# Turning cached keys in 32x32 blocks on VectorE, and dividing by the row sums after P·V instead of before it

## The reference

```python
kc = k_cache[block_table].reshape(bsz, L, HK, D)
k_all = jnp.concatenate([kc, k], axis=1)
scores = jnp.einsum('bqhd,bkhd->bhqk', q, k_all) * SCALE
scores = jnp.where(valid[:, None, None, :], scores, -1e+30)
probs = jax.nn.softmax(scores, axis=-1)
o = jnp.einsum('bhqk,bkhd->bqhd', probs, v_all)
return jnp.einsum('bse,de->bsd', o.reshape(bsz, seqlen, HQ * D), Wo)
```

## Time and profile before

| | |
|---|---|
| median of 3 runs | 1533.02 us |
| the profiled execution, own time | 1530.62 us |
| its span | 1528.9 us |
| PE / VectorE / ScalarE / GpSimd busy | 94% / 76% / 61% / 32% of the span |
| mean granted TensorE clock | 0.992 |
| layer 1, its 66 steps | about 300 to 1466 us of the span |
| cached keys turned on PE | 256 matmuls, 38.7 us busy |
| P divided: ScalarE / VectorE | 128 x 0.824 us / 128 x 0.545 us |

### The profile page before, as it was taken

The page is one execution under the profiler, slowest core; times in us unless marked ns, Lnnn a source line. Parts: engine busy times, 40 slices in busy tenths (PEclk is TensorE's granted clock), DMA queues, the critical chain, the costliest instruction groups (busy, mean ns, idle before and its releaser), DMA issues.

```text
span 1528.9 us, 29324 instructions
## 1 busy us (share of the span) xinstructions
PE 1434.5 (94%) x8014; PEld 1230.2 (80%) x8014; DVE 1163.2 (76%) x2800; ACT 939.4 (61%) x1860; POOL 493.7 (32%) x678
## 2 busy tenths in 40 slices
PE   3998999788999899999999999999999999999988
PEld 2776887667788788888878887888788888888767
DVE  4675767566688788778878886888788778888756
ACT  2333232356677677767767776777677667777643
POOL 4243000155543333333433333343333333433200
PEclk9999999999999999999999999999999999999999
DMA  8678642345321112111111111021112111111214
GB/s 179 207 240 283 197 150 89 98 126 159 111 63 49 50 29 63 60 40 49 50 47 45 57 56 51 29 63 49 51 29 63 60 40 49 50 42 36 97 60 161
DMA packets 104275, 131.03 MB, mean 86 GB/s; under 512 B 11861, under 2 KB 79590, under 8 KB 98838
## 3 DMA queue, kind: packets, MB, share of 16 engines
q1 hardware_dynamic: 98678, 109.49, 23.6%
q0 software_dynamic: 5024, 17.93, 3.9%
q10 hardware_dynamic: 384, 1.41, 0.7%
HBM read 125.63 MB, written 36.72 MB: 106 GB/s over the span
## 4 chain that ended last, share of the span: by engine, by line
PE 75%; issue 9%; DVE 7%; ACT 2%; POOL 2%; DMA 2%; POOLq 1%; SPq 1%; ACTq 0%; DVEq 0%
PE proj_ps L1170 16%; PE sc L1210 12%; PE o_ps L1247 12%; PE proj_ps L1268 11%; PE ring L1229 8%; PE proj_ps L1026 4%; PE o_ps L1026 4%; PE sc L1026 3%; PE ring L1283 2%; PE ring L1295 1%; PE ring L1026 1%; DMA wd_raw<-in_WdT 1%; POOLq L584 1%; DVE w_l L1426 1%; POOL v_pages L585 1%
## 5 line engine op out<-in xcount | busy, mean ns | idle before, releaser
L1699 DVE TENSOR_TENSOR pTl<-ring,pTh 128x512 fp32r<-128x512 f32 x320 | 215.1, 689 | 72.8 <-ACT pTh L851 69.3
L833 ACT ACTIVATE p_sb<-p_sb,bias,rstd 128x640 f32<-128x640 f32 x256 | 235.8, 921 | 46.7 <-DVE bias L1675 46.7
L637 POOL TENSOR_TENSOR rstd<-var,half_neg 128x4 f32<-128x4 f32 x64 | 80.6, 1259 | 532.1 <-DVE var L1736 483.5
L851 ACT ACTIVATE pTh<-ring 128x512 fp32r<-128x512 f32 x320 | 184.4, 599 | 55.2 <-PE ring L1229 54.4
L1665 DVE CUSTOM_DVE_ANT_0 p_sb<-sc,mask 128x640 f32<-128x640 f32 x256 | 209.1, 817 | 4.4 <-PE sc L1210 0.8
L1229 PE MATMUL ring<-ident,p_sb 128*128 128x128 f32 x1280 | 183.5, 274 | 5.7 <-DVE p_sb L1691 3.4
L1170 PE MATMUL proj_ps<-wh,xh 128*128 128x512 f32 (+1 forms) x512 | 179.7, 351 | 8.9 <-issue 8.2
L1229 PEld LDWEIGHTS ring<-ident,p_sb 128*128 128x128 f32 x1280 | 153.9, 141 | 33.5 <-DVE p_sb L1691 3.7
L1170 PE MATMUL proj_ps<-wl,xh 128*128 128x512 f32 (+1 forms) x512 | 172.6, 337 | 0.0
L1170 PE MATMUL proj_ps<-wh,xl 128*128 128x512 f32 (+1 forms) x512 | 172.2, 336 | 0.0
L1210 PE MATMUL sc<-kTh,qTh 128*128 128x320 f32 x512 | 163.5, 319 | 1.8 <-DVE kTl L1800 1.8
(11 more groups left out here) (247 smaller groups left out, 3632.7 us busy)
## 6 DMA issues: line engine op xcount, KB each, us to landing
k_pages<-in_k_cache SPq DMA_DIRECT2D x128, 128.0 KB, 3.4
v_pages<-in_v_cache POOLq DMA_DIRECT2D x128, 128.0 KB, 3.5
k_raw<-k_pages SPq DMA_DIRECT2D x64, 256.0 KB, 3.1
v_raw<-v_pages SPq DMA_DIRECT2D x64, 256.0 KB, 3.0
stage<-in_Wqkv SPq DMA_DIRECT2D x32, 384.0 KB, 3.5
w_raw<-in_WguT SPq DMA_DIRECT2D x20, 512.0 KB, 5.7
stage<-in_WoT SPq DMA_DIRECT2D x32, 256.0 KB, 3.3
w_raw<-in_W3T SPq DMA_DIRECT2D x8, 1024.0 KB, 5.4
```

The source lines that it names most:

```text
L833: act_e.activation(p_sb[:, p_slot(u, h), :], p_sb[:, p_slot(u, h), :], ACT.Exp, bias=bias[:, h:h + 1], scale=rstd[:, u.k % 2, h:h + 1], ac ...
L851: act_e.activation(pTh[:, c, :], ring[c % 2][:, :], ACT.Copy).then_inc(S["pth"], 1)
L1699: v.tensor_tensor(pTl[:, c, :], ring[c % 2][:, :], pTh[:, c, :].bitcast(F32), ALU.subtract).then_inc(S["ptl"], 1)
```

## The change

The keys are loaded by four DMAs instead of one, so that key 32·i + c, dimension 32·j + r lies at partition 32·j + c, column 32·i + r: `k_raw` is [128, 512], and one 32x32 block-wise transpose on VectorE (`turn_cached_k`) gives the full transpose in `k_turned`. PE's `transpose_keys` is gone, its semaphore `kcT` now comes from VectorE; the low part of the cached keys moves from VectorE to GpSimd. P is no longer divided: `invert` makes one reciprocal of four columns, SyncE writes it to DRAM with heads and tokens swapped and reads it back onto all partitions (`spread_inv`), and VectorE multiplies the unit's `o_ps` by that row (`norm_o`) into `o_sb`, which shares memory with `q_sin`. `oTh` and `oTl` are made from `o_sb`.

SyncE, `load_k`, `spread_inv` and `step`:

```diff
-                sp.dma_start(k_raw[:, :, :], of_head(k_pages, u)).then_inc(k_load, 16)
+                pages = k_pages[u.seq, :, :, :].rearrange("(i r) h d -> r i (h d)", r=PSIZE)
+                for j in range(D // PSIZE):
+                    sp.dma_start(k_raw[j * PSIZE:(j + 1) * PSIZE, :].rearrange("r (i c) -> r i c", c=PSIZE),
+                                 pages[:, :, bass.ds(u.head * D + j * PSIZE, PSIZE)]).then_inc(k_load, 16)
...
+            def spread_inv(u):
+                if not u.exists():
+                    return
+                par = u.k % 2
+                sp.wait_ge(S["inverted"], u.count(1, 1))
+                sp.dma_start(inv_dram[par].rearrange("h t -> t h"), inv[:, par, :],
+                             allow_slow_non_contiguous=True).then_inc(S["inv_put"], 16)
+                sp.wait_ge(S["inv_put"], u.count(16, 16))
+                sp.dma_start(inv_row[:, :], inv_dram[par].rearrange("h t -> (h t)").partition_broadcast(P)
+                             ).then_inc(S["inv_in"], 16)
...
                 if u.exists() and (u.turn is not None or u.k > 0):
                     load_k(u)
+                spread_inv(u + -2)
                 load_in(u + 4, 0)
```

GpSimd, `turn_and_norm`:

```diff
+                if u.back(3):
+                    pool.wait_ge(S["ol"], (u + -3).count(1, 1))
...
+                pool.wait_ge(S["kch"], u.count(1, 1))
+                pool.tensor_tensor(kTl[:, u.k % 2, 0:L], k_turned[:, :], kTh[:, u.k % 2, 0:L].bitcast(F32), ALU.subtract
+                                   ).then_inc(S["kcl"], 1)
                 pool.wait_ge(S["q_var"], u.count(1, 1))
```

ScalarE (both `normalise` calls are gone, and `high_cached_k` stands ahead of `square_q`):

```diff
-                act_e.wait_ge(S["pv"], u.count(KC, KC))
+                act_e.wait_ge(S["on"], u.count(1, 1))
...
-                act_e.activation(oTh[:, :], o_ps[:, :], ACT.Copy).then_inc(S["oh"], 1)
+                act_e.activation(oTh[:, :], o_sb[:, :], ACT.Copy).then_inc(S["oh"], 1)
...
-                act_e.activation(kTh[:, u.k % 2, 0:L], ring[1][:, :], ACT.Copy).then_inc(S["kch"], 1)
+                act_e.activation(kTh[:, u.k % 2, 0:L], k_turned[:, :], ACT.Copy).then_inc(S["kch"], 1)
```

PE (`transpose_keys` is gone):

```diff
-                    pe.wait_ge(S["normed_v"], u.count(2, 2))
-                    pe.wait_ge(S["normed_s"], u.count(2, 2))
+                    pe.wait_ge(S["exped"], u.count(REP, REP))
```

VectorE:

```diff
+            def norm_o(u):
+                if not u.exists():
+                    return
+                dve.wait_ge(S["pv"], u.count(KC, KC))
+                dve.wait_ge(S["inv_in"], u.count(16, 16))
+                if (u + 2).exists():
+                    dve.wait_ge(S["qrope"], (u + 2).count(1, 1))
...
+                v.tensor_tensor(o_sb[:, :], o_ps[:, :], inv_row[:, :], ALU.mult).then_inc(S["on"], 1)
...
+                dve.wait_ge(k_load, u.count(4 * 16, 4 * 16))
...
+                v.transpose(k_turned[:, :], k_raw[:, :]).then_inc(S["kcT"], 1)
```

More of the change, by code:

```diff
@@ L234, in cond_resid_kernel @@
         sq_q = l1_sb("sq_q", [P, QW])
-        sq_k = l1_sb("sq_k", [P, D])
+        sq_k = sq_q[:, 0:D]
         q_cos = l1_sb("q_cos", [P, QW])
@@ L252, in cond_resid_kernel @@
         bias = l1_sb("bias", [P, 8])
-        total = l1_sb("total", [P, 8])
-        inv = l1_sb("inv", [P, 8])
+        total = l1_sb("total", [P, 2, REP])
+        inv = l1_sb("inv", [P, 2, REP])
+        inv_row = l1_sb("inv_row", [P, QW])
+        o_sb = q_sin
+        k_turned = l1_sb("k_turned", [P, L])
         l1.close()
@@ L1270, in output @@
                 i.then_inc(S["y"], 1)
-            def transpose_keys(u):
-                if not u.exists():
-                    return
-                pe.wait_ge(k_load, u.count(16, 16))
-                if u.back(2):
-                    pe.wait_ge(S["ptl"], (u + -2).count(KC, 4))
-                elif u.k == 0:
-                    pe.wait_ge(S["x1l"], HALF)
-                else:
-                    pe.wait_ge(S["knl"], u.count(1, 0))
-                for c in range(LC):
-                    i = nc.tensor.transpose(ring[1][:, c * P:(c + 1) * P], k_raw[:, c, :], ident[:, :])
-                i.then_inc(S["kcT"], 1)
             def transpose_queries(u):
@@ L1705, in low_o @@
                 dve.wait_ge(S["oh"], u.count(1, 1))
-                v.tensor_tensor(oTl[:, :], o_ps[:, :], oTh[:, :].bitcast(F32), ALU.subtract).then_inc(S["ol"], 1)
+                v.tensor_tensor(oTl[:, :], o_sb[:, :], oTh[:, :].bitcast(F32), ALU.subtract).then_inc(S["ol"], 1)
             def add_y(u):
@@ L1829, in step @@
                 new_wo(u + -2, 2)
-                low_cached_k(u)
                 new_wo(u + -2, 3)
+                norm_o(u + -2)
                 scale_k(u)
@@ L1835, in step @@
                 low_q(u)
-                invert(u + -1, 1)
                 low_new_k(u)
```

70 lines of the change are left out of this document (29 added, 41 removed).

## The result

The changed kernel takes **2022.08 us** (median of 4 runs, 2020.62 to 2025.97), the kernel before 1533.60 in the same session: a ratio of **1.318 (1.316 to 1.321)**. The forecast was 1551.8, with 1524 to 1590 as its range. The sign was right, the size was not: +489 us where +18.8 were forecast. The profiled execution has a span of 2020.3 us.

The account below looks back on a forecast made before the run. PE's issue, busy 94% of the span, and lateness of results it waits for bound the kernel. Terms 3.1 + 3.2 + 16.8 - 2.4 - 1.9 = +18.8 us on 1533.02 gave 1551.8 us, range 1524 to 1590.

Parts of the forecast that it names:

- The inverses: Write and read through DRAM: ready at 984.5, wanted by `norm_o` at 988.1, so 3.6 us of play for the write.
- the write of the inverses is slow: Rival: 4-byte pieces, sixteen neighbours to 64 bytes, delay `norm_o` each step; 1680 us at 8.5 us landing; chance 0.10.
- PE's transposes: Ordinary step: PE loses four key transposes, 0.44 us, but then waits for chunk 4 of P; -0.12 us a step.
- (b): Ordinary step: VectorE's key transpose stands ahead of chunk 2's subtraction, so PE turns chunk 4 later; +0.05 us a step.
- The block transpose: VectorE's transpose of the keys: taken as 0.60 us of the engine, bounded by 0.28 and 1.20.
- (c): Ordinary step: way from P·V to the output product grows by `norm_o`, 2.59 instead of 2.45 us; +0.14 us.
- GpSimd's new subtraction: GpSimd's subtraction for the keys' low part: 1.29 us, lying in its idle time.
- Early steps: Five early steps where GpSimd copies pages: `norm_o` stands behind `sum_k`, +0.6 us each, +3.2 us in all.
- New Wo pieces: Seven steps: piece 3 is issued later on SyncE and split right before `norm_o`; +2.4 us each, +16.8 us (+3 to +28).
- Loop turns: Where the loop turns, ScalarE's wait for key transposes goes: -0.4 us six times, -2.4 us.
- The end: Last steps: PE's 3.4 us of waits for divided P go, `norm_o` adds 0.75 to each of two outputs; -1.9 us.
- The relief of VectorE and ScalarE: Fewer divisions on both engines and fewer reciprocals on VectorE: neither was waited for there, so worth nothing.

Follow-up runs that it names:

- v_first: Changed kernel with its slow write; SyncE issues the values and Wo piece before waiting for the write, the read of the inverses behind them: 1918.2 us.
- turn_first: Changed kernel; VectorE turns the inverses by blocks, four DMAs write 128-byte pieces, values issued before the wait for the write: 1570.0 us, 1.024 of the kernel before.
- keys_alone: Kernel before with only the keys' part: four key DMAs, block transpose on VectorE, low part on GpSimd; P divided as before: 1540.7 us, 1.0035.
- keys_last: Kernel before plus keys' part; GpSimd's subtraction waits for the scaled key, keys turned behind P's last chunk, ScalarE's high part after the output copy: 1522.0 us, 0.9900.
- full_late: Changed kernel; inverses turned, 128-byte pieces, values before the write's wait, keys turned behind P's last chunk, GpSimd held until the key is scaled: 1570.1 us, 1.022.
- keys_krope: Kernel before plus keys' part, GpSimd's subtraction of the keys held back until VectorE has scaled the new key: 0.9962 of the kernel before.
- turn_inv: Changed kernel; VectorE turns the inverses by 32x32 blocks, four DMAs write them in 128-byte pieces, values still behind the wait: 1583.0 us, 1.031 of the kernel before.

## Why the prediction was wrong, point by point

**The inverses: the step that failed.** "Write and read cost two landings of at least the 3.1 us of the earlier trace rows and two issues of 0.4, so 984.5 ... The write may take 3.6 us longer than a usual load before anyone notices." What failed is the price of the write, taken as that of a usual load. It takes 8.9 to the issue of the read instead of 3.5, and the read lands in 5.5 instead of 3.1: 14.4 us in place of 7.0, so 7.4 more where the play was 3.6. The rival "the write of the inverses is slow" was right in its mechanism, that neighbouring 4-byte pieces make it slow; it had 0.10, and the range left it out. The argument against it, 3.6 us of play, was no evidence about the write. The Trainium skill's rule ("DMA: Bandwidth & Descriptors", "Specifications": read-modify-write below 512 bytes) stood on its side, but gives no price, and 4-byte pieces 64 bytes apart, as far below 512, landed in 1.9 us. So that rule alone does not tell the slow write from the quick one.

**Its price** was wrong as well: 1680 at 8.5 us. "1.8 x 57" counts a delay once a step, as if each step began on time. The inverses begin when the output product of the step before is added, so the step becomes as long as the whole ring, 23.7 us in the one shown. Not in the sum either: the values queued behind the wait (1.5 us a step, `v_first`), loads that land together (6.2 us instead of 3.0 for the values), and the output product at half clock (1.55). The text did ask what stands behind the wait for the write, but only for the Wo steps.

**The rest can be read from the kernels with a quick write** (`turn_first`, 1.024):

- *PE's transposes, "0.12 of 0.44 us is left"*, and *(b) +0.05*: together -0.07 us; measured 17.28 to 17.18 in `keys_alone`, -0.10, in three ordinary steps of four (the fourth, behind new Wqkv, is 0.29 longer until GpSimd is held back). Right. The 0.32 that were held back come not free in `keys_last` either (17.13), as the argument on chunk 4 had it.
- *The block transpose, 0.60 us of the engine*: 0.70 us as a row, 0.63 of the engine in all 64. Right; the estimate of 1.24 from the Trainium skill's 128x128 bf16 figure was nearly twice too high for this shape, and the measurement decides.
- *(c) `norm_o`, +0.14*: +0.34 (17.18 to 17.52). The mis-sized term is VectorE's answer to PE, put at the 0.42 us of the addition to x: behind the last matmul of P·V it is 0.62, in `turn_first` and, with nothing in front of it, in `full_late`. Why the two answers differ stays open.
- *"GpSimd's new subtraction (1.29 us ...) lies in its idle time"*: GpSimd was idle, but VectorE was held up meanwhile. What that cost is 0.7%, the step from `keys_alone` to `keys_krope`, and it fell in the early steps, those with new Wo and the one behind new Wqkv.
- *Early steps, +3.2*: first eight +8.4 in `turn_first`; +3.3 are the keys' part and go to -1.0 once GpSimd is held back.
- *New Wo pieces, +2.4 each*: +3.6 in `turn_first`, +3.1 with pieces 64 bytes apart. In that run the order is as forecast, and the links are near it: piece 3 is issued 7.0 us behind piece 2 (6.7 forecast), ScalarE has it 4.4 later (4.1), and PE begins 3.45 behind ScalarE (3.45). Piece 3 issued behind the read and the values, ScalarE, VectorE, `norm_o`, `oTl`:

```profile
787.92 0.35 SPq L524 DMA_DIRECT2D inv_row<-scale_dram  x1
788.44 0.39 SPq L461 DMA_DIRECT2D v_raw<-v_pages  x1
789.02 0.35 SPq L470 DMA_DIRECT2D stage<-in_WoT  x1
...
793.39 0.63 ACT L762 ACTIVATE woh<-stage 128x512 fp32r<-128x512 f32 x1 [2.31 <-DMA stage<-in_WoT]
...
794.06 0.69 DVE L1564 TENSOR_TENSOR wol<-stage,woh 128x512 fp32r<-128x512 f32 x1 [1.37 <-ACT woh L762]
794.67 0.68 DVE L1709 TENSOR_TENSOR q_sin<-o_ps,inv_row 128x512 f32<-128x512 f32 x1
...
796.05 0.69 DVE L1715 TENSOR_TENSOR oTl<-q_sin,oTh 128x512 fp32r<-128x512 f32 x1 [0.50 <-ACT oTh L888]
```

- *New Wqkv pieces*: no term; +1.3 us each (17.72 to 19.02). In `full_late` it is +0.57, so over half goes with GpSimd's wait and the place of the transpose.
- *Loop turns, -2.4 in all*: the two steps of a turn went from 38.8 to 37.1 in `turn_first`, -1.7 each time. But -0.8 came with the keys' part alone, and `turn_inv`, which differs from `turn_first` only in issuing the values behind the wait as the change does, has 39.0. So with the change's own order nothing is left of the gain, and the rest of the -1.7 is the values' earlier issue, which the forecast did not contain.
- *The end, -1.9*: +1.5 in `turn_first` (the last seven steps take 119.0 us instead of 117.5).
- *The relief of VectorE and ScalarE "is worth nothing"*: no run shows a gain from it. Each loses 128 divisions, and the fastest kernel of all, `keys_last`, still has them.

So even with a quick write the change is 2.4% slower, twice the 1.2% forecast. The sign came out right for the reasons given only in part: the steps with new Wo were in the sum, those with new Wqkv were not.

## What to carry to other kernels

Before a new transfer goes into a loop, look at the addresses of its pieces, not only their number, and write out which event of the last step starts it: if the way leads back through what waits for it, a delay isn't added once but sets the step. Look for every new instruction on GpSimd at the durations of the VectorE operations that it meets, also those with a single SBUF tensor, and not only the first one: one wait that keeps them apart was worth 0.7% here, one that only moved the meeting nothing. And a remedy found under one bound must be tried again under the next: taking the inverses early gained 154 us under the slow write and lost 44 without it.

## What was not expected of the hardware

- One write of 512 pieces of 4 bytes to neighbouring addresses of DRAM: 8.9 us; 16 bytes apart 2.7; 64 bytes apart 1.93; as 128 pieces of 16 bytes side by side 1.74.
- VectorE operations with their tensors in SBUF that meet a GpSimd subtraction of 1.30 us: 0.28 became 1.40 us (128x128, two tensors), 0.28 became 1.43 (128x128, one tensor and a scale), 0.96 became 2.00 (128x768, two tensors). The 128x512 block transpose and operations with an operand in PSUM were not held up.
- A stride of 16 bytes in the SBUF operand of a 128x512 multiplication (the other in PSUM): 0.69 us became 1.08.
- The 128x32 block transpose takes 0.21 us, the 128x512 one 0.70.
- After a stretch of 5.4 us with PE busy for 1.05, a clock of 0.51 for the 3 us looked at, then 1.00.
